# H split into a high and a low part as it leaves PSUM, stored as a pair and loaded straight into the operand ring; edges in 125 rows, loaded first; adjacency total on VectorE

## The chip, the core and the metric

The program runs on one core of a Trainium2 chip. The metric is the time of one execution in device microseconds (us). Three executions of the kernel before took 1498.07, 1499.3 and 1508.9 us; the median is 1499.3 us.

## The reference

A graph of 625 nodes with 1024 features goes through two layers; 20,625 edges (source, destination, one of 8 types) are given as three lists. What matters here is the first part, a relational graph convolution with a gate:

```python
x = x + L0_gnn(layernorm(x))        # this part
x = x + int8_ffn(layernorm(x))
x = x + gcn(layernorm(x))           # uses the sum of all adjacencies
x = x + mixture_of_experts(layernorm(x))

def L0_gnn(x):
    out = x @ root + bias
    for r in range(8):
        mask = (edge_type == r)
        sums = segment_sum(x[src] * mask, dst)
        cnt = segment_sum(mask, dst)
        out = out + (sums / max(cnt, 1)) @ weight[r]
    z = concat([out, x]) @ w_gate + b_gate
    return tanh(out) * z + x * (1 - z)
```

## The kernel before, in words

The mean over the edges and the product with a weight are exchanged. For each relation r, H_r = x @ weight[r] (625 x 1024) is computed first; then the adjacency of r (625 x 625, counts of edges) is multiplied by H_r, and each row is scaled by one over its count.

All f32 products run as products of numbers in the fp32r format. An operand is split in a high part (a copy to fp32r) and a low part (the rest); weights need three matmuls (high x high, low x high, high x low), the adjacency, whose numbers are small integers, needs two. The 625 nodes are 5 chunks of 125 rows, which stand on 125 partitions. Moving operands are tiles of 512 columns. A tile arrives by DMA in `stage` (two halves of up to four tiles, one DMA for each half, line 381), ScalarE copies its high part into `rh` (L330), VectorE subtracts and writes the low part into `rl` (L338). `rh` and `rl` are a ring of RT = 10 tiles: tile i may be written when tile i-10 has been used by TensorE.

**First stage, the units (L532 to L541).** Unit 0 is the root weight, units 1 to 8 the relations, unit 9 the gate's second half. A unit has two half-units (512 columns of the result each); a half-unit is 8 weight tiles x 5 chunks x 3 = 120 matmuls. Its five results stand in five of the eight PSUM banks. For units 1 to 8 ScalarE copies each to one of NHE = 6 slots `He` (L975), and its queue stores the slot in DRAM, `h_scratch` (L979). Unit 9 is added to a bias by VectorE (L1276), stored in `zx_scratch`, and read back later.

**Beside it: the edges.** The three edge lists are loaded by ScalarE's queue in pieces of 83, 78 and 1 rows (L939 to L941). Keys (destination, type, source as one number) are made from them, turned by TensorE, stored in DRAM, and read back in windows of 640 keys, each copied to 128 partitions (`KR`, L924). In each half-unit VectorE compares two windows (L1210, L1213), and GpSimd adds 165 columns of counts into `adj_scratch` in DRAM by indirect DMAs (L1759), in groups of five; a group waits for the one before it.

**Second stage, the spreads (L567 to L583).** For each relation and half, 5 tiles of H are loaded from `h_scratch` through `stage` (L381), split by ScalarE and VectorE, and multiplied with the adjacency, in 50 matmuls. The adjacency of a relation is loaded into `acb` (L396), copied by ScalarE into `Ar` (L934), and summed over sources by VectorE (L1289). GpSimd sums the eight adjacencies into `Atot` by eight DMAs that add (L1765). VectorE adds the scaled results to `U` (L1322). SP's queue issues all loads in program order.

After that come the gate (whose weights are loaded at the end of the second stage), the int8 layer, the second graph layer and the experts; the change doesn't touch them.

Of the kernel before, what the change touches and what calls it, by code (L numbers as in the profile page):

```python
# [17 lines left out]
P, C = 125, 5  # L18
# [5 lines left out]
KROWS = 83  # L24
EDGES0 = KROWS * 128
# [84 lines left out]
def gnn_ffn_kernel(nc, x, src, dst, typ, w_root, w_rel, w_gate, w_gnn, w_e1, w_e2, w_s1, w_s2, w_int8,  # L110
                   rbias, gbias, wscale, fbias, nbias, router, b1, b2, out):
    hd = nc.dram_tensor("h_scratch", (R, 2, P, C * 512), F32, kind="Internal").ap()
    zxd = nc.dram_tensor("zx_scratch", (2, P, C * 512), F32, kind="Internal").ap()
    xed = nc.dram_tensor("xe_scratch", (NSP, D), F32, kind="Internal").ap()
    eod = nc.dram_tensor("eo_scratch", (NS7 + 128, D), F32, kind="Internal").ap()
    keyd = nc.dram_tensor("key_scratch", (2 * KROWS, 128), F32, kind="Internal").ap()
# [5 lines left out]
    with ExitStack() as ctx:  # L122
# [19 lines left out]
        rh = sb("rh", [128, RT, 512], F32R)  # L142
        rl = sb("rl", [128, RT, 512], F32R)
# [40 lines left out]
        er = [sb(f"er{i}", [KROWS, 2, 128], I32, ph0) for i in range(3)]  # L184
        kr0 = sb("kr0", [KROWS, 2, 128], F32, ph0)
        kr1 = sb("kr1", [KROWS, 2, 128], F32, ph0)
        kc = sb("kc", [128, TILES], F32, ph0)
        KR = sb("KR", [128, 4, TG * 128], F32, ph0)
        EQ = sb("EQ", [128, TG, TG * 128], BF16, ph0)
        later = sb("later", [128, (2 * TG - 1) * 128], BF16, ph0)  # L190
        cnt = sb("cnt", [128, TILES], F32, ph0)
        kd1 = sb("kd1", [128, TILES], F32, ph0)
        idx = sb("idx", [128, TILES], I32, ph0)
        dum = sb("dum", [128, TG], F32, ph0)
        Z = sb("Z", [128, 1527], F32, ph0)
        sb("hole0", [128, 9875 + C * N - 5 * 256 - 4 * TILES - 4 * TG * 128 - TG * TG * 64 - (2 * TG - 1) * 64 - TG - 1527], F32, ph0)
        He = sb("He", [P, NHE, 512], F32, ph0)
# [71 lines left out]
        d_tot = count("adj_totalled", 16)  # L269
        d_zx, d_xl = count("zx_in", 16), count("x_again", 16)  # L270
# [8 lines left out]
        banks = Banks()  # L279

# [16 lines left out]
        for r in range(R):  # L297
            for hf in range(2):
                group(hd[r, hf][:, 0:1536], P, *[("h", r, hf, k) for k in range(3)])
                group(hd[r, hf][:, 1536:2560], P, *[("h", r, hf, k) for k in range(3, 5)])  # L300
# [23 lines left out]
        def high_parts(e, on, to, split):  # L324
            for i in range(split[0], min(to, len(tiles))):
                s, h, _ = places(i)
                on.wait_ge(*at("loaded", tiles[i][0]))
                if i >= RT:
                    on.wait_ge(*at("used", i - RT))
                e.copy(h, s).then_inc(*a_hi.up(("hi", i)))  # L330
            split[0] = max(split[0], min(to, len(tiles)))

        def low_parts(e, on, to, split, own):
            for i in range(split[0], min(to, len(tiles))):
                if (i in pool_lo) == (own is p_lo):
# [16 lines left out]
        sums = [slice(0, 4 * P), slice(4 * P, N)]  # L352
# [10 lines left out]
        h_last = [("h_out", unit, hf, c) for unit in (R - 1, R) for hf in range(2) for c in range(C)]  # L363
        h_out = [("h_out", R - 1, 1, c) for c in range(2, C)] + [("h_out", R, hf, c) for hf in range(2) for c in range(C)]


        def sync(e, on):
            def load(g):
# [7 lines left out]
                if name[0] == "h":  # L376
                    for c in range(C):
                        on.wait_ge(*at("h_out", name[1], name[2], c))
# [12 lines left out]
            def adjacency_in(r):  # L391
                on.wait_ge(*at("added", TILES - 1))
                on.wait_ge(*at("slot zero"))
                if r >= 2:
                    on.wait_ge(*at("adj", r - 2))
                e.dma_start(acr[r % 2], adjacency(r)).then_inc(*d_adj[r % 2].up(("acb", r)))  # L396

            for g in range(2, first("h", 0, 0, 0)):
# [4 lines left out]
            for r in range(R):  # L403
                for g in range(first("h", r, 0, 0), first("h", r, 0, 0) + 4):
                    if r == 0 and g == first("h", 0, 1, 0):
                        adjacency_in(0)
# [1553 lines left out]
```

## Time and profile before

| | |
|---|---|
| three executions | 1498.07, 1499.3, 1508.9 us |
| profiled execution: time / span | 1508.7 / 1506.9 us |
| TensorE matmul busy | 1147.6 us (76% of the span) |
| VectorE / ScalarE / GpSimd busy | 800.1 / 400.5 / 427.8 us |
| granted TensorE clock, mean | 0.885 |
| moved by DMA | 205.7 MB, 137 GB/s over the span |
| chain that ended last | TensorE 49%, DMA 23%, VectorE 14% |

The span is cut by eye into a start (to 99.7 us), the first stage (to about 634 us), the second stage (to about 1057 us) and the rest. "DMA share" is the mean busy share of the core's 16 DMA engines, so 0.31 is what five of sixteen give. A clock of 1.00 is 2.4 GHz, 0.50 is 1.2 GHz. In the chain of waits each line is a piece of the path that ended last: start, length, what it was.

### The profile page before, as it was taken

How to read it: one execution, taken by the hardware profiler on the slowest of the kernel's cores; microseconds unless marked ns; L12 is line 12 of the kernel's file. 1: busy time of each engine (PE TensorE's matmuls, PEld its weight loads, DVE VectorE, ACT ScalarE, POOL GpSimd, SP SyncE). 2: the span in 40 equal slices, each digit the busy share in tenths (PEclk: the TensorE clock that was granted, in tenths of full speed). 3: DMA queues.
4: the chain of work that ended last, by engine and by line, in shares of the span. 5: the costliest groups of instructions: out<-in, count | busy, mean ns of one | idle time of the engine just before them, and what ended most of it. 6: DMA issues, size and time to landing. Idle time of an engine off the chain costs nothing.

```text
span 1506.9 us, 13564 instructions
## 1 busy us (share of the span) xinstructions
PE 1147.6 (76%) x5123; PEld 903.3 (60%) x5123; DVE 800.1 (53%) x1226; ACT 400.5 (27%) x672; POOL 427.8 (28%) x294
## 2 busy tenths in 40 slices
PE   0489999999999999833612555667895999779893
PEld 0367777777777777622411444556664687658772
DVE  0579677678677651121302143444489646646545
ACT  0321322322322322100101022223254423315651
POOL 1226656656556551100000000000063500230023
PEclk9999999999999999967765877888897999979996
DMA  4764567765554554553443332223320110177846
GB/s 152 269 227 110 142 178 210 202 164 150 155 148 128 145 134 111 168 146 100 98 122 85 103 114 89 105 105 134 114 75 37 70 56 29 37 202 250 269 159 166
DMA packets 95586, 205.70 MB, mean 137 GB/s; under 512 B 43845, under 2 KB 44622, under 8 KB 87066
## 3 DMA queue, kind: packets, MB, share of 16 engines
q1 hardware_dynamic: 26796, 128.69, 25.0%
q0 software_dynamic: 51568, 41.88, 14.5%
q10 hardware_dynamic: 17150, 34.19, 6.4%
q8 instruction: 44, 0.72, 0.2%
q14 instruction: 28, 0.23, 0.1%
HBM read 148.66 MB, written 55.97 MB: 136 GB/s over the span
## 4 chain that ended last, share of the span: by engine, by line
PE 49%; DMA 23%; DVE 14%; SPq 3%; ACT 3%; ACTq 3%; issue 2%; POOL 2%; another core or an unknown queue 0%; POOLq 0%; DVEq 0%
PE ps L479 43%; DMA stage<-h_scratch 14%; SPq L381 3%; DMA stage<-in_w_e 3%; DVE rl L338 3%; ACTq L940 2%; DMA acb<-adj_scratch 2%; DVE U L1322 2%; DVE Sr L1289 2%; ACT Ar L934 1%; PE ps L740 1%; DVE st L1161 1%; PE ps L703 1%; DMA xe_scratch<-U,SI 1%; DMA G<-eo_scratch,SI 1%
## 5 line engine op out<-in xcount | busy, mean ns | idle before, releaser
L338 DVE TENSOR_TENSOR rl<-stage,rh 128x512 fp32r<-128x512 f32 (+1 forms) x330 | 220.9, 710 | 493.3 <-ACT rh L330 492.8
L330 ACT CAST rh<-stage 128x512 fp32r<-128x512 f32 (+1 forms) x344 | 203.9, 622 | 765.4 <-DMA stage<-h_scratch 336.9
L479 PE MATMUL ps<-rh,xTh 128*125 128x512 f32 x880 | 351.1, 399 | 11.3 <-DVE rl L338 8.7
L479 PE MATMUL ps<-rl,xTh 128*125 128x512 f32 x880 | 349.3, 397 | 0.0
L479 PE MATMUL ps<-rh,xTl 128*125 128x512 f32 x880 | 347.9, 395 | 0.0
L1759 POOL DMA_INDIRECT adj_scratch<-cnt,idx x165 | 277.7, 1683 | 233.8 <-DMA adj_scratch<-cnt,idx 87.0
L479 PE MATMUL ps<-rh,Ar 125*125 125x512 f32 x400 | 177.0, 442 | 40.1 <-DVE He L1276 28.7
L479 PEld LDWEIGHTS ps<-rh,xTh 128*125 128x125 f32 x880 | 164.5, 187 | 54.5 <-DVE rl L338 10.0
L479 PEld LDWEIGHTS ps<-rh,xTl 128*125 128x125 f32 x880 | 164.3, 187 | 42.5
L479 PEld LDWEIGHTS ps<-rl,xTh 128*125 128x125 f32 x880 | 164.3, 187 | 40.3
L479 PE MATMUL ps<-rl,Ar 125*125 125x512 f32 x400 | 172.6, 432 | 0.0
L554 PE MATMUL ps<-ones,Sr 125*125 125x2 f32 x40 | 9.1, 337 | 171.4 <-DVE Sr L1289 171.4
L1210 DVE SCALAR_TENSOR_TENSOR EQ<-KR,kc,later 128x640 bf16<-128x640 f32 x165 | 134.1, 878 | 0.0
L479 PEld LDWEIGHTS ps<-rh,Ar 125*125 125x125 f32 x400 | 84.7, 212 | 67.3 <-DVE He L1276 29.4
L1213 DVE TENSOR_REDUCE cnt<-EQ 128x5 f32<-128x3200 bf16 x33 | 115.1, 3487 | 1.1
L554 PEld LDWEIGHTS ps<-ones,Sr 125*125 125x125 f32 x40 | 8.6, 306 | 174.5 <-DVE Sr L1289 174.4
L1765 POOL DMA_DIRECT2D Atot<-adj_scratch x8 | 23.0, 2871 | 268.0 <-DMA Atot<-adj_scratch 203.1
L479 PEld LDWEIGHTS ps<-rl,Ar 125*125 125x125 f32 x400 | 84.0, 210 | 20.9 <-issue 0.3
L1778 POOL TENSOR_TENSOR ZX<-ZX,U 125x512 f32<-125x512 f32 x5 | 9.7, 1943 | 195.8 <-DVE U L1364 195.8
L975 ACT COPY He<-ps 125x512 f32<-125x512 f32 x80 | 46.9, 587 | 28.7 <-ACT He L975 13.6
L1322 DVE SCALAR_TENSOR_TENSOR U<-ps,rc,U 125x512 f32<-125x512 f32 x75 | 51.1, 744 | 5.1 <-PE ps L479 4.3
L338 POOL TENSOR_TENSOR rl<-stage,rh 128x512 fp32r<-128x512 f32 x14 | 17.5, 1273 | 85.7 <-ACT rh L330 85.7
(264 smaller groups left out, 1333.6 us busy)
## 6 DMA issues: line engine op xcount, KB each, us to landing
stage<-in_w_rel SPq DMA_DIRECT2D x32, 1024.0 KB
h_scratch<-He ACTq DMA_DIRECT2D x80, 250.0 KB
stage<-in_w_e SPq DMA_DIRECT2D x16, 1024.0 KB
adj_scratch<-Z POOLq DMA_DIRECT2D x16, 763.5 KB, 25.4
Atot<-adj_scratch POOLq DMA_DIRECT2D x8, 1525.9 KB, 40.3
acb<-adj_scratch SPq DMA_DIRECT2D x8, 1525.9 KB
stage<-h_scratch SPq DMA_DIRECT2D x16, 750.0 KB
KR<-key_scratch ACTq DMA_DIRECT2D x33, 320.0 KB
```

What stands on the lines that cost most here:

```text
L330: e.copy(h, s).then_inc(*a_hi.up(("hi", i)))
L338: e.tensor_tensor(l, s, h.bitcast(F32), ALU.subtract).then_inc(*own.up(("lo", i)))
L381: e.dma_start(stage[0:rows, g % 2, 0:n * 512], source).then_inc(*d_group[g % 2].up(("loaded", g)))
L479: ins = e.matmul(ps[0:P, b, :], a, m, start=first and n == 0, stop=last and n == len(parts) - 1)
L940: e.dma_start(er[i][0:78, 1, :], a[EDGES0:20608].rearrange("(p q) -> p q", q=128)).then_inc(*d_edge.up())
L975: e.copy(He[:, s % NHE, :], ps[0:P, banks.of["unit", unit, hf, c], :]).then_inc(*a_out.up(("he", unit, c, hf)))
L1210: e.scalar_tensor_tensor(out=EQ[:, j, :], in0=KR[:, g % 4, :], scalar=kc[:, t:t + 1], in1=later[:, j0:j0 + TG * 128], op0=ALU.is_equal, op ...
L1213: e.tensor_reduce(cnt[:, cols], EQ[:], AX, ALU.add).then_inc(*v_row.up(("cnt", g)))
L1289: e.tensor_tensor(Sr[:, r % 2, :], a[:, 0, :] if c == 1 else Sr[:, r % 2, :].bitcast(F32), a[:, c, :], ALU.add).then_inc(*v_row.up(("sourc ...
L1322: e.scalar_tensor_tensor(out=U[:, c, HALF[hf]], in0=ps[0:P, banks.of["spread", r, hf, c], :], scalar=rc[:, r, c:c + 1], in1=U[:, c, HALF[h ...
L1759: e.indirect_dma_start(accd, bass.IndirectOffsetOnAxis(ap=idx[:, n:n + 1], axis=0), cnt[:, n:n + 1], None, compute_op=ALU.add).then_inc(*d ...
L1765: e.dma_start(Atot[:], adjacency(r), accum_op=ALU.add if r else ALU.bypass).then_inc(*d_tot.up(("total", r)))
```

## The change

- H is split as it leaves PSUM: ScalarE copies the high part into slot `Hp[:, s, 0]`, VectorE subtracts it from the PSUM bank and writes the low part into `Hp[:, s, 1]`, and ScalarE's queue stores both, 4 KB in each of 125 rows, in `h_scratch`, which is twice as large. In ScalarE's program the five copies of a half-unit come first, then the five stores.
- The loads of H no longer pass `stage`: one DMA for each tile puts both parts into slot i % 10 of `ring` (`rh` and `rl` are its two halves), when tile i-10 has been used. ScalarE and VectorE do nothing for these tiles.
- Unit 9 is not stored in DRAM; VectorE leaves it in `He` or in `stage`, and ScalarE copies it to `ZX`. The gate's first weights are loaded in relations 3 and 4.
- The copy of adjacency 0 comes after all units in ScalarE's program, no longer ahead of the last half-unit.
- The edges are 125 rows of 165, the first three DMAs of SP's queue; x goes out in turns on SP's and ScalarE's queues. A window is 625 keys on 125 partitions.
- `Atot` is summed by VectorE from `acb` (seven additions of 125 x 3125); GpSimd's eight DMAs are gone. The load of adjacency r+1 goes out between the two halves of relation r.

```diff
-            for c in range(C):
+            for i, a in enumerate((src, dst, typ)):
+                e.dma_start(er[i][:], a.rearrange("(p t) -> p t", p=TK)).then_inc(*d_edge.up(("edges",)))
+            for c in (0, 2, 4):
                 e.dma_start(U[:, c, :], x_v[:, c, :]).then_inc(*d_x[c].up(("x", c)))
-                if c in (0, 1):
-                    load(c)
+                if c < 4:
+                    load(c // 2)
...
+            def h_in(r, hf):
+                for k in range(C):
+                    i = tile["h", r, hf, k]
+                    on.wait_ge(*at("h_out", r, hf, k))
+                    on.wait_ge(*at("used", i - RT))
+                    e.dma_start(ring[0:P, i % RT, :, :].bitcast(F32).rearrange("p a n -> p (a n)"), h_part(r, hf, k)).then_inc(*d_h[i % RT].up(("lo", i)))
...
+            h_in(0, 0)
+            adjacency_in(0)
+            adjacency_in(1)
+            h_in(0, 1)
+            for r in range(1, R):
+                h_in(r, 0)
+                if r + 1 < R:
+                    adjacency_in(r + 1)
+                h_in(r, 1)
...
-                    for c in range(C):
-                        if unit and unit <= R:
+                    if unit and unit <= R:
+                        for c in range(C):
                             on.wait_ge(*at("unit", unit, hf, c))
-                            if s >= NHE:
-                                on.wait_ge(*at("he slot", s - NHE))
-                            e.copy(He[:, s % NHE, :], ps[0:P, banks.of["unit", unit, hf, c], :]).then_inc(*a_out.up(("he", unit, c, hf)))
-                        if unit:
-                            to = (hd[unit - 1, hf] if unit <= R else zxd[hf]).rearrange("p (c n) -> p c n", c=C)
+                            if s + c >= NHE:
+                                on.wait_ge(*at("he slot", s + c - NHE))
+                            e.copy(Hp[:, (s + c) % NHE, 0, :], ps[0:P, banks.of["unit", unit, hf, c], :]).then_inc(*a_out.up(("he high", unit, c, hf)))
+                        for c in range(C):
                             on.wait_ge(*at("he", unit, c, hf))
-                            e.dma_start(to[:, c, :], He[:, s % NHE, :]).then_inc(*d_he[s % NHE].up(("he slot", s), ("h_out", unit - 1, hf, c)))
+                            e.dma_start(h_part(unit - 1, hf, c), Hp[:, s % NHE, :, :].bitcast(F32).rearrange("p a n -> p (a n)")).then_inc(
+                                *d_he[s % NHE].up(("he slot", s), ("h_out", unit - 1, hf, c)))
                             s += 1
...
+                        elif unit <= R:
+                            on.wait_ge(*at("he high", unit, c, hf))
+                            e.tensor_tensor(Hp[:, s % NHE, 1, :], ps[0:P, b, :], Hp[:, s % NHE, 0, :].bitcast(F32), ALU.subtract).then_inc(
+                                *v_out.up(("he", unit, c, hf)))
...
+            def add_total(r):
+                on.wait_ge(*at("acb", r - 1))
+                on.wait_ge(*at("acb", r))
+                if r > 1:
+                    on.wait_ge(*at("total", r - 1))
+                e.tensor_tensor(Atot[:].rearrange("p c i -> p (c i)"), acb[0][:] if r == 1 else Atot[:].rearrange("p c i -> p (c i)"), acb[r % 2][:],
+                                ALU.add).then_inc(*v_row.up(("total", r)))
...
-            for r in range(R):
-                on.wait_ge(*(at("total", r - 1) if r else at("added", TILES - 1)))
-                e.dma_start(Atot[:], adjacency(r), accum_op=ALU.add if r else ALU.bypass).then_inc(*d_tot.up(("total", r)))
```

ScalarE's queue at the end of a half-unit of the first stage, before (`He` are the slots, `h_scratch` is DRAM, `KR` the windows of keys, `rh` the ring's high parts):

```order
L975 COPY He<-ps 125x512 [waits h_out4,products_done]
L979 DMA h_scratch<-He 125x512 [waits act_evicted]
L975 COPY He<-ps 125x512 [waits h_out5,products_done]
L979 DMA h_scratch<-He 125x512 [waits act_evicted]
L975 COPY He<-ps 125x512 [waits h_out0,products_done]
L979 DMA h_scratch<-He 125x512 [waits act_evicted]
L975 COPY He<-ps 125x512 [waits h_out1,products_done]
L979 DMA h_scratch<-He 125x512 [waits act_evicted]
L975 COPY He<-ps 125x512 [waits h_out2,products_done]
L979 DMA h_scratch<-He 125x512 [waits act_evicted]
L330 CAST rh<-stage 128x512
L924 DMA KR<-key_scratch 128x640 [waits dve_done]
```

The same place now:

```order
L988 CAST Hp<-ps 125x512 [waits h_out4,products_done]
L988 CAST Hp<-ps 125x512 [waits h_out5,products_done]
L988 CAST Hp<-ps 125x512 [waits h_out0,products_done]
L988 CAST Hp<-ps 125x512 [waits h_out1,products_done]
L988 CAST Hp<-ps 125x512 [waits h_out2,products_done]
L991 DMA h_scratch<-Hp 125x1024 [waits dve_evicted] x5
L336 CAST ring<-stage 128x512
L935 DMA KR<-key_scratch 125x625 [waits dve_done]
```

The stores carry 1024 columns for 512, they wait for VectorE, and the load of the keys has 125 rows for 128.

SP's queue in the second stage, before (two halves of a relation and the adjacency of the one after next):

```order
L381 DMA stage<-h_scratch 125x1536 [waits h_out4,dve_low_parts,h_out5,act_high_parts,h_out0,h_out1,h_out2]
L381 DMA stage<-h_scratch 125x1024 [waits act_high_parts,dve_low_parts]
L381 DMA stage<-h_scratch 125x1536 [waits h_out3,dve_low_parts,h_out4,act_high_parts,h_out5,h_out0,h_out1]
L381 DMA stage<-h_scratch 125x1024 [waits act_high_parts,dve_low_parts]
L396 DMA acb<-adj_scratch 125x5x625 [waits act_done]
```

And now, one relation:

```order
L411 DMA ring<-h_scratch 125x1024 [waits products_done,h_out4]
L411 DMA ring<-h_scratch 125x1024 [waits products_done,h_out5]
L411 DMA ring<-h_scratch 125x1024 [waits products_done,h_out0]
L411 DMA ring<-h_scratch 125x1024 [waits products_done,h_out1]
L411 DMA ring<-h_scratch 125x1024 [waits products_done,h_out2]
L404 DMA acb<-adj_scratch 125x5x625 [waits dve_done,act_done]
L411 DMA ring<-h_scratch 125x1024 [waits products_done,h_out3]
L411 DMA ring<-h_scratch 125x1024 [waits products_done,h_out4]
```

The loads wait for TensorE (`products_done`) where they waited for the splitting engines, each tile has a DMA of its own, and a relation loads 10 x 125 x 1024 columns for 10 x 125 x 512.

## Rows read from the trace of the kernel before

**Rows 1.** The page, DMA issues: transfers, count, KB each, us to landing.

```profile
stage<-in_w_rel SPq DMA_DIRECT2D x32, 1024.0 KB
h_scratch<-He ACTq DMA_DIRECT2D x80, 250.0 KB
...
Atot<-adj_scratch POOLq DMA_DIRECT2D x8, 1525.9 KB, 40.3
acb<-adj_scratch SPq DMA_DIRECT2D x8, 1525.9 KB
stage<-h_scratch SPq DMA_DIRECT2D x16, 750.0 KB
KR<-key_scratch ACTq DMA_DIRECT2D x33, 320.0 KB
```

**Rows 2.** Windows: stretch, length, engines busy (instructions), clock, DMA share, GB/s.

```profile
12.00:36.00 24.00, 0.00 (x0) 0.00 (x0) 0.00 (x0) 0.00 (x0) 0.00 (x0) 1.00 0.32 129
52.00:58.00 6.00, 4.02 (x13) 3.06 (x12) 4.71 (x8) 3.22 (x6) 4.16 (x8) 1.00 1.03 373
99.70:627.00 527.30, 527.27 (x2261) 420.44 (x2262) 351.81 (x418) 136.11 (x225) 279.48 (x166) 1.00 0.56 154
408.00:463.40 55.40, 55.40 (x239) 44.17 (x239) 41.38 (x48) 15.78 (x26) 30.65 (x19) 1.00 0.53 144
584.00:604.00 20.00, 20.00 (x88) 15.97 (x87) 4.97 (x9) 3.56 (x6) 0.00 (x0) 1.00 0.32 130
634.00:1057.00 423.00, 210.17 (x791) 162.37 (x791) 130.57 (x212) 71.44 (x96) 20.11 (x11) 0.72 0.37 110
929.00:1046.00 117.00, 89.10 (x349) 70.78 (x349) 54.74 (x87) 29.60 (x39) 0.00 (x0) 0.83 0.29 109
```

**Rows 3.** Windows within a half-unit, while the stores of H are in flight.

```profile
444.00:446.00 2.00, 2.00 (x10) 1.61 (x9) 2.00 (x1) 0.07 (x1) 0.83 (x1) 1.00 0.33 127
```

**Rows 4.** Windows in the second stage, loads of adjacency and H.

```profile
974.00:978.00 4.00, 4.00 (x19) 3.20 (x18) 0.00 (x0) 0.11 (x1) 0.00 (x0) 1.00 0.32 129
...
982.00:986.00 4.00, 4.00 (x19) 3.15 (x19) 2.84 (x5) 0.00 (x0) 0.00 (x0) 1.00 0.32 126
```

**Rows 5.** Chain of waits, the start: start, length, what.

```profile
28.79 10.96 ACTq L940
39.78 5.43 DMA er<-in_typ
...
54.65 2.41 DVE rl L338 x4
```

**Rows 6.** Chain of waits, end of the second stage.

```profile
1040.22 10.67 DMA stage<-h_scratch
...
1053.27 4.28 PE ps L479 x10
...
1059.02 9.83 DMA stage<-in_w_gate
...
1071.02 1.90 PE ps L469 x8
...
1077.45 2.33 PE ps L479 x10
```

**Rows 7.** Single lines: duration ns min/median/max, first and last start.

```profile
L979 ACTq DMA_DIRECT2D h_scratch<-He x80: 256/277/4568, 155.1 to 578.2; - x80
L338 DVE TENSOR_TENSOR rl<-stage,rh x330: 677/685/1771, 54.6 to 1451.1; 128x512 fp32r<-128x512 f32 x125, 125x512 fp32r<-125x512 f32 x40
```

**Rows 8.** The page, costliest groups, an eviction on VectorE: busy, mean ns; idle before.

```profile
L1322 DVE SCALAR_TENSOR_TENSOR U<-ps,rc,U 125x512 f32<-125x512 f32 x75 | 51.1, 744 | 5.1 <-PE ps L479 4.3
```

**Rows 9.** The scatter-adds of GpSimd: the line, and its longest idle time.

```profile
L1759 POOL DMA_INDIRECT adj_scratch<-cnt,idx x165: 1541/1548/2188, 96.3 to 566.1; - x165
...
  DMA adj_scratch<-cnt,idx: 87.0, 20
```

More of the change, by code:

```diff
@@ L23 @@
 TG = 5
-KROWS = 83
-EDGES0 = KROWS * 128
+TK = E // TILES
 NG = TILES // TG
@@ L141, in gnn_ffn_kernel @@
         stage = sb("stage", [128, 2, SW], F32)
-        rh = sb("rh", [128, RT, 512], F32R)
-        rl = sb("rl", [128, RT, 512], F32R)
+        ring = sb("ring", [128, RT, 2, 512], F32R)
+        rh, rl = (ring[:, :, i, :] for i in range(2))
         EOs = sb("EOs", [HC, 3, D], F32, phx)
@@ L298, in gnn_ffn_kernel @@
             for hf in range(2):
-                group(hd[r, hf][:, 0:1536], P, *[("h", r, hf, k) for k in range(3)])
-                group(hd[r, hf][:, 1536:2560], P, *[("h", r, hf, k) for k in range(3, 5)])
+                for k in range(C):
+                    tile["h", r, hf, k] = len(tiles)
+                    tiles.append((None, 0, P))
         for hf in range(2):
@@ L334, in low_parts @@
             for i in range(split[0], min(to, len(tiles))):
-                if (i in pool_lo) == (own is p_lo):
+                if tiles[i][0] is not None and (i in pool_lo) == (own is p_lo):
                     s, h, l = places(i)
@@ L375, in load @@
                             on.wait_ge(*at("lo", i))
-                if name[0] == "h":
-                    for c in range(C):
-                        on.wait_ge(*at("h_out", name[1], name[2], c))
+                if name[0] == "gate" and g <= tiles[tile["gate", 0, 4]][0]:
+                    on.wait_ge(*at("zx copied", 1))
                 if g in (tiles[tile["e1", 2, 0]][0], tiles[tile["e2", 0, 0, 0]][0]):
@@ L519, in tensor @@
             nothing = lambda c: None
[L522 to L528 removed]
+            b, freed = banks.take(("keys",), ("key rows",))
+            on.wait_ge(*at("key columns"))
+            on.wait_ge(*at("ident"))
+            for ev in freed:
+                on.wait_ge(*at(*ev))
+            e.transpose(ps[:, b, 0:TK], kc[:, 0:128], ident[0:TK, 0:TK]).then_inc(*product.up())
+            e.transpose(ps[0:TILES - 128, b, TK:2 * TK], kc[:, 128:TILES], ident[0:TK, 0:TK]).then_inc(*product.up(("keys turned",)))
             banks.drop(("keys",))
@@ L960, in scalar @@
                 for hf in range(2):
-                    if unit == R + 1 and hf == 1:
-                        adjacency_copy(0)
                     if unit or hf:
@@ L993, in scalar @@
+            for hf in range(2):
+                for c in range(C):
+                    on.wait_ge(*at("he", R + 1, c, hf))
+                    on.wait_ge(*at("unit", R + 1, 1, C - 1))
+                    e.copy(ZX[:, c, HALF[hf]], zx_place(c, hf)).then_inc(*a_row.up(("zx copied", hf)))
+            for r in range(R):
+                if r + 1 < R:
+                    adjacency_copy(r + 1)
+                if 3 <= r <= 7:
+                    c = r - 3
                     on.wait_ge(*at("x again"))
@@ L1345, in vector @@
                 many_vector(e, Waiter(e))
-            lows(tile["h", R - 1, 1, 0] + RT)
+            lows(tile["gate", 0, 5])
             for c in range(C):
```

189 lines of the change are left out of this document (80 added, 109 removed).

## The prediction

> **What bounds the kernel now.** I read the windows first, then the sizes of the transfers, then the chain of waits, and the single lines last.
>
> In the first stage TensorE is busy without a gap: 2261 matmuls in 527.3 us, 0.233 us each, so 27.7 to 28 us for a half-unit's 120 [rows 2]. In the second it is busy 210 of 423 us, at a mean clock of 0.72, while the DMA share is 0.37 at 110 GB/s [rows 2]. That looks like idle DMA engines. It isn't. The reader should put three windows side by side: 12 to 36 us, where only x and the two biases (125 rows each) are on their way, runs at a share of 0.32 and 129 GB/s; 584 to 604, loads and stores of H together, 0.32 and 130 GB/s; 52 to 58, with 128-row transfers, 1.03 and 373 GB/s [rows 2]. In the middle of the first stage, stores of H: 0.33, 127 [rows 3]. In the second, adjacency and H: 0.32 to 0.33 at 126 to 129 [rows 4]. So everything with 125 rows goes through five of the sixteen engines, at about 130 GB/s together whichever queue it comes from, and mixing loads and stores or queues adds nothing. The account to keep is that of these five.
>
> In the steady first stage the mean engine works 0.53 x 27.7 = 14.7 us of a half-unit [rows 2]. H's store is 5 x 250 KB = 1.28 MB [rows 1], 9.85 us on five engines, 3.1 as a mean of sixteen. The rest, 11.6 us, lies on all (weights, windows of keys, scatter-adds). The five have 9.85 + 11.6 = 21.5 us of work in 27.7. In the last three relations of the second stage, 117 us [rows 2], a relation takes 39 us and holds 2.56 + 1.56 MB [rows 1], 31.7 us at 130 GB/s: 81% busy.
>
> **The start.** The keys wait for the edges until 45.2 us, through the slow issue of the pieces on ScalarE's queue [rows 5]; the fourth low part ends at 57. Now the edges are first, 0.25 MB, and should be there by 8 us. Then x and weights bound the start: ahead of the second weight group the five engines carry the edges, x chunks 0 and 2, and 1 and 3 from the other queue, 2.3 MB or 18 us, and two weight groups, 2.1 MB at 373 GB/s or 6 us; it lands at about 27 us, and was used at about 60. I take 30 us saved; the ends are 0 (ScalarE caught in the issue of its two loads) and 37 (x chunk 0 alone decides).
>
> **The first stage.** H's store doubles: 2.56 MB, 19.7 us on the five. The windows of keys had 128 rows, 0.66 MB at 373 GB/s, 1.8 us of every engine; now they have 125, 0.62 MB at 130, 4.8 us of the five. New load of the five in a half-unit: 19.7 + 11.6 - 1.8 + 4.8 = 34.3 us, where TensorE wants 27.7. Six slots of H hold a little over one half-unit, so the excess soon reaches the PSUM banks. VectorE isn't the bound: it is busy 41.4 in two half-units, 20.7 in one [rows 2], and gets 5 subtractions more, at the price of an eviction, 0.744 us [rows 8], 3.7 us: 24.4 of 27.7. ScalarE waits for them before it stores, but has a whole half-unit of tiles split ahead.
>
> The first store was issued at 155.1 [rows 7], now at 125. Fifteen intervals of 34.3 us and a last batch of 19.7 us give 659 us for the last store. TensorE alone would have issued that batch at 125 + 15 x 27.7 = 540.
>
> **The second stage.** What the five still have to move then: H, 2 x 20.5 = 41 MB at 130 GB/s, 315 us; eight adjacencies, 12.5 MB, 98 us; x again, 2.56 MB, 20 us; two groups of gate weights, 6 us. Sum 439 us. The first loads of H may go out while TensorE is in its last half-unit, and the ring has room for ten tiles, so I let the five run through: the last tile of H lands at 659 + 439 = 1098. At full clock TensorE needs 800 x 0.233 = 186 us there and at half clock (ten in 4.28 against 2.33 us [rows 6]) 342; neither bounds. VectorE loses 80 low parts of 0.685 us [rows 7] and gets seven additions, which I bound from five lines of the eviction's kind, 5 x 0.744 = 3.7 us, 26 us in all, under cover of the loads. GpSimd's eight adding DMAs, 40.3 us each [rows 1], go. Relations with them beside took (929 - 634) / 5 = 59 us, those without 39 [rows 2], so this removal is worth up to 100 us; H's doubling takes it back: a relation is now 5.12 + 1.56 MB, 51.4 us at 130 GB/s.
>
> **The end.** The last load of H landed at 1050.9; two chunks of matmuls later, and after 13.5 us for gate weights, the first turn came at 1071.0 [rows 6]. Now these weights are there: last landing, 4.3 + 3.7 us of matmuls, turn. The rest, 1506.9 - 1071.0 = 436 us, is unchanged. Span = 1098 + 8 + 436 = 1542, with 1.8 us around it 1544, against the profiled execution's 1508.7: +35. Against the median of 1499.3 that is 1535.
>
> **A rule of the skill against the rows.** The Trainium skill, "DMA: Bandwidth & Descriptors", section "Issuing engines are not separate DMA queues", says that DMAs of all queues run on the same 16 engines, and its section "Measured (HBM→SBUF, 128 partitions, SWDGE, issued from GpSimd)" has 341 GB/s for 1 MB. Taken alone these would hide H's doubling. The same page, section "Why a DMA increments its semaphore by 16 and not by 1", says that the number of engines is the largest up to 16 that divides the outer dimensions on both sides; for 125 that is 5. By that rule the trace agrees: 0.32 of 16 is five [rows 2].
>
> **Rivals.**
> - *All sixteen carry the new transfers* (the first rule above). Units end at 634 - 30 = 604, the second stage is TensorE's 186 us: 604 + 186 + 8 + 436, 1226 on the median's scale. Against it stand all windows of rows 2 to 4. Chance 0.02.
> - *Faster: the first stage stays TensorE's.* The five would have to do 34.3 us of work in 27.7, say because rows of 4 KB move faster than those of 2 KB. Units end at 604, loads of H start 35 us earlier: last landing 569 + 439 = 1008, span 1452, on the median's scale 1445. It decides at a load of 27.7 us, 160 GB/s on five engines; x has rows of 4 KB and ran at 129 [rows 2]. Chance 0.12.
> - *Slower still: the scatter-adds are late.* A group is 5 x (1.548 + 0.3) = 9.3 us of issue and a wait, 87 us over 20 waits before [rows 9]; first to last start, 470 us for 33 groups, 14.2 us each. A half-unit of 34.3 us allows 17.1. If the waits grow in engines that are never free, to 20 us a group, they end at about 70 + 660 = 730, and the adjacency, on which SP's queue stands with H behind it, was due at 665: +65, 1600. Chance 0.12.
> - *The start saves nothing:* the first store stays at 155, +30, 1565. Chance 0.10.
> - *The clock:* in gaps it falls, and 120 matmuls at half clock need 51 us, above 34.3. If it stayed there, +16 x 17. A busy TensorE got it back within a few us before. Chance 0.03.
>
> **The numbers.** My forecast has 0.61, and its own range is 1500 to 1575: 3% on a rate of 130 GB/s is 25 us, and gaps in the five's work can only add. This measurement tells about 1% from no change. Faster by over 1% (under 1484): 0.02 + 0.12 and a tail of 0.01, 0.15. Within 1% (up to 1514): the forecast's lower end, 0.15. Slower: 0.70. The range of 8 in 10 leaves out the fast rivals and the far end of the slow ones: 1475 to 1600.
>
> **What would show it.** In the changed kernel's profile: the first matmul at 20 to 27 us for 55; the first store of H near 125; in the first stage a DMA share of at least 0.5 that never falls under 0.31, gaps in TensorE where it had none, 34 us for a half-unit, and ScalarE waiting for the slots or standing in its issue of stores; the last store near 660; in the second stage a share of 0.31 to 0.33 at 130 GB/s throughout, 51 us for a relation, TensorE waiting for `ring`; the gate with no wait for weights. Wrong it would be if the share in the first stage fell to 0.31 between stores and TensorE stayed without gaps, or if H's rows moved at another rate than 130 GB/s.

## The result, and the profile after

The changed kernel takes 1732.9 us (median of 4 runs, 1725.7 to 1742.2), the kernel before, run beside it, 1504.1: a ratio of 1.152, 95% interval 1.142 to 1.162. Forecast were 1535 us, and a range of 1475 to 1600. The sign was right, the size was not: 198 us are missing.

Its profiled execution has a span of 1724.3 us. The page, its 40 slices and its queues (packets, MB, share of sixteen engines' span):

```profile
PE   2899888789889899000055535465549789897994
...
POOL 2054224232422426776600000000003540131004
PEclk8999999889999999555578967888879889997996
DMA  6845556554554553111133333333330211037846
GB/s 199 342 119 155 174 177 189 183 177 157 172 168 150 164 170 84 1 1 1 1 127 129 130 130 141 130 141 130 130 129 26 97 51 59 26 105 224 272 169 177
...
q0 software_dynamic: 81312, 29.65, 9.5%
q10 hardware_dynamic: 15132, 52.38, 7.9%
```

Look at slices 17 to 20, counted from 1. TensorE is at 0, nothing moves (1 GB/s), yet the DMA engines show a share of a tenth, and GpSimd is at its busiest, 6 and 7. Something small is late. The windows, in the columns of [rows 2]:

```profile
75.70:688.00 612.30, 554.40 (x2280) 437.52 (x2280) 396.99 (x505) 123.83 (x224) 216.90 (x104) 0.95 0.52 162
400.00:500.00 100.00, 92.41 (x385) 72.80 (x384) 72.35 (x92) 21.82 (x40) 37.05 (x18) 0.97 0.54 168
696.00:856.00 160.00, 0.00 (x0) 0.00 (x0) 0.00 (x0) 0.00 (x0) 114.51 (x59) 0.50 0.15 1
900.00:950.00 50.00, 27.27 (x102) 19.67 (x103) 13.69 (x17) 2.80 (x1) 0.00 (x0) 0.86 0.32 130
```

The first stage runs from 75.7 to 688 and its 2280 matmuls fill 91% of it. Then comes a hole of 160 us, in which only GpSimd works, on 59 instructions. The second stage is as forecast: 0.32 at 130 GB/s. What GpSimd does in the hole is the scatter-adds, line L1773, which answers to [rows 9]; beside it the casts that fill H's slots:

```profile
L1773 POOL DMA_INDIRECT adj_scratch<-cnt,idx x165: 1977/1986/2695, 94.3 to 857.3; - x165
its engine sat idle before it (us, times) until:
  DMA adj_scratch<-cnt,idx: 219.8, 21
  issue: 120.0, 138
```
```profile
L988 ACT CAST Hp<-ps x80: 577/597/624, 131.6 to 630.8; 125x512 fp32r<-125x512 f32 x80
```

Both begin as early as before, or earlier (94.3 for 96.3 us). But the last scatter-add is issued at 857.3 us, where it was 566.1 [rows 9]; one takes 1986 ns to issue for 1548, and the waits for the adding DMAs are 219.8 us for 87.0. TensorE's and ScalarE's first stage was over some 170 us earlier. The chain of waits through the hole (start, length, what) repeats one pattern, the issues of a group, 0.3 us apart, and then a wait of 3.6 us:

```profile
746.19 3.63 DMA adj_scratch<-cnt,idx
...
750.67 1.99 POOL adj_scratch L1773
752.65 0.30 issue
752.96 1.98 POOL adj_scratch L1773
...
759.82 3.55 DMA adj_scratch<-cnt,idx
```

A group of five takes 759.82 - 746.19 = 13.6 us there, with nothing else running. While H is being stored it costs more than twice that. GpSimd in order of time (start, length, what, idle before it and its releaser):

```profile
408.60 1.98 POOL L1773 DMA_INDIRECT adj_scratch<-cnt,idx  x1 [0.30 <-issue]
429.42 1.99 POOL L1773 DMA_INDIRECT adj_scratch<-cnt,idx  x1 [18.83 <-DMA adj_scratch<-cnt,idx]
...
439.68 1.99 POOL L1773 DMA_INDIRECT adj_scratch<-cnt,idx  x1 [0.30 <-issue]
462.39 1.98 POOL L1773 DMA_INDIRECT adj_scratch<-cnt,idx  x1 [20.72 <-issue]
```

From 429.42 to 462.39 is one group: 33 us. The releaser of the second wait is given as "issue", but it lies at the same place of the loop, before the first scatter-add of a group, where the program waits for the group before. From the first store of H to the last the mean of 14 groups is 32.9 us; over the whole run it is (857.3 - 94.3) / 32.8 = 23.3 us, for 14.3 before (32 whole groups and the four issues of the last make 32.8).

Did VectorE deliver the counts too late? A group needs its indices, which VectorE writes. Their lines, before and after (first and last start):

```profile
L1219 DVE TENSOR_TENSOR idx<-kd,dum x33: 164/166/168, 95.9 to 543.3; 128x5 int32<-128x5 f32 x33
```
```profile
L1233 DVE TENSOR_TENSOR idx<-kd,dum x33: 164/165/196, 71.8 to 601.4; 125x5 int32<-125x5 f32 x33
```

Now the last indices are written at 601.4 us and the last scatter-add goes out 256 us later, so VectorE isn't the cause. Before, the first twenty groups each started within some 3 us of their indices, which came every (543.3 - 95.9) / 32 = 14.0 us. The 14.3 us of before are for the most part VectorE's pace, not the price of a group.

Who waits for the last scatter-add is SyncE. The first adjacency is issued at 860.9, and all but five of H's loads stand behind it (the queue of SyncE: start, time until the last of the row is issued, what, how many):

```profile
655.26 14.26 SPq L411 DMA_DIRECT2D ring<-h_scratch  x5
```
```profile
860.89 5.10 SPq L404 DMA_DIRECT2D acb<-adj_scratch  x2
910.33 3.50 SPq L404 DMA_DIRECT2D acb<-adj_scratch  x1
913.92 47.66 SPq L411 DMA_DIRECT2D ring<-h_scratch  x10
961.63 3.54 SPq L404 DMA_DIRECT2D acb<-adj_scratch  x1
```

From one adjacency to the next it is 961.63 - 910.33 = 51.3 us: a relation's price in the forecast was 51.4. (The next one, which also loads x, takes 71.3, the two with gate weights 55.7 and 57.0, the last 51.4.) The end of that stage in the chain of waits, which answers to [rows 6]:

```profile
1263.74 26.34 DMA ring<-h_scratch
1290.12 4.47 PE ps L488 x12
1294.59 0.85 PE ps L478 x8
1295.44 2.32 PE ps L488 x10
```

No wait for gate weights is left, as forecast.

### The profile page after: what moved, and what is told of

Same layout as the page of the kernel before. It is cut to its first block, busy times and chain, and to the rows that moved or that the text cites. A ratio compares the mean times of both kernels' runs of the same rounds, so it can differ in the third digit from the quotient of the medians.

```text
span 1724.3 us, 13452 instructions
## 1 busy us (share of the span) xinstructions
PE 1174.0 (68%) x5123; PEld 907.3 (53%) x5123; DVE 812.9 (47%) x1229; ACT 350.0 (20%) x604; POOL 465.6 (27%) x285
## 3 DMA queue, kind: packets, MB, share of 16 engines
q0 software_dynamic: 81312, 29.65, 9.5%
q10 hardware_dynamic: 15132, 52.38, 7.9%
## 4 chain that ended last, share of the span: by engine, by line
SPq 23%; DMA 21%; DVE 17%; PE 14%; POOL 12%; ACTq 5%; issue 5%; ACT 2%; POOLq 0%; DVEq 0%
SPq L411 21%; DMA adj_scratch<-cnt,idx 12%; POOL adj_scratch L1773 11%; PE ps L488 9%; ACTq L991 5%; DVE EQ L1224 3%; DVE ring L344 3%; DVE cnt L1227 3%; DMA stage<-in_w_e 2%; SPq L404 2%; DMA ring<-h_scratch 2%; DVE Hp L1284 1%; PE ps L751 1%; PE ps L714 1%; DMA G<-eo_scratch,SI 1%
## 5 line engine op out<-in xcount | busy, mean ns | idle before, releaser
L488 PE MATMUL ps<-ring,xTh 128*125 128x512 f32 x1760 | 573.6, 408 | 71.0 <-DVE Hp L1284 56.5
L488 PE MATMUL ps<-ring,Ar 125*125 125x512 f32 x800 | 229.1, 439 | 383.1 <-issue 192.4
L1773 POOL DMA_INDIRECT adj_scratch<-cnt,idx x165 | 339.7, 2059 | 475.1 <-DMA adj_scratch<-cnt,idx 219.8
L488 PEld LDWEIGHTS ps<-ring,xTh 128*125 128x125 f32 x1760 | 336.7, 193 | 161.6 <-DVE Hp L1284 62.0
L488 PEld LDWEIGHTS ps<-ring,Ar 125*125 125x125 f32 x800 | 159.3, 207 | 448.8 <-DMA ring<-h_scratch 219.7
L488 PE MATMUL ps<-ring,xTl 128*125 128x512 f32 x880 | 354.5, 403 | 0.0
L344 DVE TENSOR_TENSOR ring<-stage,ring 128x512 fp32r<-128x512 f32 x250 | 167.3, 717 | 238.8 <-ACT ring L336 233.4
L336 ACT CAST ring<-stage 128x512 fp32r<-128x512 f32 x264 | 153.4, 624 | 554.7 <-issue 183.7
L488 PEld LDWEIGHTS ps<-ring,xTl 128*125 128x125 f32 x880 | 169.0, 192 | 44.1
L1224 DVE SCALAR_TENSOR_TENSOR EQ<-KR,kc,later 125x625 bf16<-125x625 f32 x165 | 131.6, 867 | 0.0
L1227 DVE TENSOR_REDUCE cnt<-EQ 125x5 f32<-125x3125 bf16 x33 | 112.5, 3408 | 1.1
```

Of the source, the lines that this page charges most:

```text
L344: e.tensor_tensor(l, s, h.bitcast(F32), ALU.subtract).then_inc(*own.up(("lo", i)))
L488: ins = e.matmul(ps[0:P, b, :], a, m, start=first and n == 0, stop=last and n == len(parts) - 1)
L1224: e.scalar_tensor_tensor(out=EQ[:, j, :], in0=KR[:, g % 4, :], scalar=kc[:, t:t + 1], in1=later[:, j0:j0 + TG * TK], op0=ALU.is_equal, op1 ...
L1227: e.tensor_reduce(cnt[:, cols], EQ[:], AX, ALU.add).then_inc(*v_row.up(("cnt", g)))
L1773: e.indirect_dma_start(accd, bass.IndirectOffsetOnAxis(ap=idx[:, n:n + 1], axis=0), cnt[:, n:n + 1], None, compute_op=ALU.add).then_inc(*d ...
```

## The experiments

Four kernels form a square: the rows of the scatter-adds (125 or 128) by the rows in which H is stored and loaded (125 or 128). Rows added to reach 128 hold zeros, and the scatter-adds' extra rows add zero to dummy places. The edits are the same throughout.

**Scatter-adds in 128 rows.** The changed kernel, with three more rows for the scatter-adds alone:

```diff
-        cnt = sb("cnt", [TK, TILES], F32, ph0)
+        cnt = sb("cnt", [128, TILES], F32, ph0)
...
-        idx = sb("idx", [TK, TILES], I32, ph0)
+        idx = sb("idx", [128, TILES], I32, ph0)
...
+            e.memset(cnt[:], 0.0).then_inc(*p_row.up())
+            e.tensor_copy(idx[:].rearrange("p (g t) -> p g t", t=TG), dum[:].unsqueeze(1).broadcast_to([128, NG, TG])).then_inc(*p_row.up(("pad rows",)))
```

> The changed kernel, with the scatter-adds in 128 rows again (three rows add 0 to places of their own); H still moves in 125 rows. Theory A (the five engines are so full of H's stores that each group of scatter-adds waits about 20 us for its last landing): a group still has parts on the five full engines, so groups stay near 30 us while H is stored, the last scatter-add starts later than 750 us, and the time stays over 1640 us. Theory B (a scatter-add in 125 rows is slow by itself, since it runs on five engines and takes 2.06 us to issue instead of 1.68): groups return to about 14 us, the last scatter-add starts before 600 us, and the time falls by about 190 us to 1540.

Measured: 1540.0 us, ratio to the kernel before 1.021 (1.016 to 1.026). Three rows more in 165 small DMAs give back 193 us. The line of the scatter-adds:

```profile
L1777 POOL DMA_INDIRECT adj_scratch<-cnt,idx x165: 1532/1542/2179, 94.5 to 658.6; - x165
its engine sat idle before it (us, times) until:
  DMA adj_scratch<-cnt,idx: 183.8, 25
```

The last one goes out 198.7 us earlier, and the issue is back at 1542 ns. The adjacency is asked for at 666.4 (forecast 665), when SyncE has issued the first five loads of H. H's last landing is at 1075.6 + 25.7 = 1101.4 (forecast 1098), the span is 1536.3 (forecast 1542). This is the kernel that my sum described. Of the two theories B had the time, and neither had the scatter-adds: the last one starts at 658.6, where A said later than 750 and B before 600.

**H in 128 rows.** The changed kernel, its scatter-adds left at 125 rows, H's tiles and its place in memory with 128 rows:

```diff
-    hd = nc.dram_tensor("h_scratch", (R, 2, P, C * 1024), F32, kind="Internal").ap()
+    hd = nc.dram_tensor("h_scratch", (R, 2, 128, C * 1024), F32, kind="Internal").ap()
...
-        Hp = sb("Hp", [P, NHE, 2, 512], F32R, ph0)
+        Hp = sb("Hp", [128, NHE, 2, 512], F32R, ph0)
```

> The changed kernel, with H stored and loaded in 128 rows (three of zeros), so that it should use all sixteen engines; scatter-adds still in 125 rows. Theory A: the five engines are free, the waits of the groups shrink to a few us, the last scatter-add starts before 640 us; the units take 28 us for a half-unit and end near 610; the second stage is bound by TensorE or by the adjacency on five engines, 190 to 230 us; time 1250 to 1330 us. Theory B: groups stay at 25 to 30 us, the last scatter-add starts after 800 us, and the second stage begins only there: time about 1500 us.

Measured: two runs, 29 us apart, 1359 and 1388 us, so no ratio is given; the trace is of the longer one. The last scatter-add is at 656.5 us, with an issue of still 1987 ns. Theory A had forecast it before 640 and the time at 1250 to 1330, theory B after 800 and about 1500: neither fits, A is the nearer. So the lateness has two causes.

**Both.**

> Both edits: H and the scatter-adds in 128 rows. Both theories: the scatter-adds are done before the units end (about 610 us), the second stage takes 190 to 230 us, and the time is 1240 to 1320 us. Theory A expects no more than 15 us between this and H in 128 rows alone; theory B expects some 200 us.

Measured: 1317.7 us, ratio 0.873 (0.870 to 0.877), last scatter-add at 554.1. The change that was 15% slower has become one that is 13% faster, with the same arithmetic. Against this kernel either cause alone makes the last scatter-add 102 to 105 us later, and both together 303, about 100 more than the sum of the two: each makes the other worse. Between this kernel and the one before it theory A expected no more than 15 us and B some 200; measured are 41 and 70.

**The kernel before, scatter-adds in 125 rows.** It leaves out the edges in the last three rows:

```diff
-                e.indirect_dma_start(accd, bass.IndirectOffsetOnAxis(ap=idx[:, n:n + 1], axis=0), cnt[:, n:n + 1], None,
+                e.indirect_dma_start(accd, bass.IndirectOffsetOnAxis(ap=idx[0:P, n:n + 1], axis=0), cnt[0:P, n:n + 1], None,
```

> The kernel before, with its scatter-adds in 125 rows instead of 128; the edges of the last three rows of each column are left out of the adjacency, nothing else differs. The price of the rows by themselves, with H's stores on the five engines at half of the changed kernel's size. Theory A: issue grows from 1.68 to 2.06 us, waits by a few us; a group takes 14 to 17 us instead of 14.2, and the time moves by less than 40 us. Theory B: a group takes 25 us or more, the last scatter-add starts after 800 us, and the time rises by over 150 us.

Measured: 1614.8 us, ratio 1.070 (1.066 to 1.075), last scatter-add at 710.9. That is 106 us more, where theory A had less than 40 and theory B over 150. The 125 rows do harm without anything else of the change, beside stores of H of half the size. The square, with the kernel before and this one below it:

```
rows of scatter / of H      last scatter-add   mean group   time
125 / 125 (the change)      857.3 us           23.3 us      1733 us
128 / 125                   658.6              17.2         1540
125 / 128                   656.5              17.1         1359 and 1388
128 / 128                   554.1              14.0         1318
before, 128 / 125, H once   566.1              14.3         1504 to 1512
before, 125 / 125, H once   710.9              18.7         1615
```

**The total alone.** The kernel before, with the seven additions on VectorE and without GpSimd's eight adding DMAs:

```diff
-            for r in range(R):
-                on.wait_ge(*(at("total", r - 1) if r else at("added", TILES - 1)))
-                e.dma_start(Atot[:], adjacency(r), accum_op=ALU.add if r else ALU.bypass).then_inc(*d_tot.up(("total", r)))
...
+                e.tensor_tensor(Atot[:].rearrange("p c i -> p (c i)"), acb[0][:] if r == 1 else Atot[:].rearrange("p c i -> p (c i)"), acb[r % 2][:],
+                                ALU.add).then_inc(*v_row.up(("total", r)))
```

> The kernel before, with the total of the adjacencies summed by VectorE and without GpSimd's eight adding DMAs: one part of the change alone. If these DMAs are what made the first five relations take 59 us instead of 39, the gain is near 100 us: 1400 to 1430. If the relations are slow there for another reason (stores of unit 9, H and adjacency on five engines), the gain is under 50 us: over 1455.

Measured: 1427.7 us, ratio 0.944 (0.941 to 0.948), 84 us less than the 1511.7 beside it. That is the part of the change worth having; the forecast gave it "up to 100". Against it the 128 / 125 kernel, which has all of the change but the 125 rows of the scatter-adds, stands at 1.021: the ratios differ by 0.077, or 116 us. So the rest of the change took back at least that, and what the start saves (24 us) on top. The rest is H's doubling and also the windows of keys in 125 rows, which in the forecast's account add 4.8 - 1.8 = 3.0 us to the five engines' half-unit, where the doubling adds 9.85. No run parts the two.

**H in 128 rows in the kernel before,** once alone and once with the total on VectorE:

```diff
-    hd = nc.dram_tensor("h_scratch", (R, 2, P, C * 512), F32, kind="Internal").ap()
+    hd = nc.dram_tensor("h_scratch", (R, 2, 128, C * 512), F32, kind="Internal").ap()
...
-        He = sb("He", [P, NHE, 512], F32, ph0)
+        He = sb("He", [128, NHE, 512], F32, ph0)
```

> The kernel before, with H stored and loaded in 128 rows, one f32 number for each element as before. The five engines' account says that 20.5 MB each way leave them: a relation without GpSimd's DMAs beside it falls from 39 to 28 to 32 us, the others from 59 to 45 to 50, the time to 1390 to 1440. If the time is not a matter of five engines, it stays within 20 us of 1504.

> The kernel before with both: H in 128 rows and the total on VectorE. It has neither H's doubling nor the early edges. If doubling H pays for itself by taking the split off ScalarE and VectorE, this is over 1385; if it doesn't, this is at 1318 + 24 (start) + 13 (gate weights), 1355 or below.

Measured: 1414.1 us (0.935, 0.932 to 0.939) and 1366.0 (0.903, 0.900 to 0.907). The first is inside its forecast of 1390 to 1440. Together the two edits save 146 us and not 98 + 84 = 182: what they relieve overlaps. It isn't the five engines alone: while GpSimd's adding DMAs of 125 rows were on their way, the share in the kernel before rose above what five of sixteen can give:

```profile
640.00:660.00 20.00, 0.00 (x0) 0.00 (x0) 1.87 (x3) 1.66 (x3) 0.00 (x0) 0.50 0.69 161
```

The second kernel lies between the two theories' numbers and decides for neither. With the earlier start (24 us) and without the wait for gate weights (13.5 us in the prediction) it would be at about 1328, an estimate; the 128 / 128 kernel, which stores and loads twice the bytes of H, has 1318. So with H in 128 rows its doubling costs nothing that shows.

**Everything on sixteen engines.** The 128 / 128 kernel, with the windows of keys in 128 rows too, and adjacency, x and biases each as a DMA of 112 rows and one of 13:

```diff
...
-                e.dma_start(acr[r % 2], adjacency(r)).then_inc(*d_adj[r % 2].up(("acb", r)))
+                for a, b in ((0, 112), (112, P)):
+                    e.dma_start(acr[r % 2][a:b], adjacency(r)[a:b]).then_inc(*d_adj[r % 2].up(("acb", r)))
...
```

> The changed kernel with every large transfer made to use all sixteen engines: H, scatter-adds and windows of keys in 128 rows, adjacency, x and the first two biases in two DMAs of 112 and 13 rows. If the second stage is bound by bytes on the five engines (adjacency), a relation falls from 32 us to TensorE's 24 and the time to 1240 to 1265. If it is bound by waits (the landing of a tile, the clock after a gap), it stays near 30 us for a relation and the time at 1295 to 1315.

Measured: 1231.2 us, ratio 0.815 (0.812 to 0.818), the best of all, and 9 us under the lower end of its forecast: the second stage was bound by bytes. Its windows over the first stage and in the second:

```profile
69.80:602.00 532.20, 532.17 (x2280) 424.33 (x2281) 402.94 (x501) 138.74 (x225) 273.08 (x164) 1.00 0.66 192
...
600.00:780.00 180.00, 177.68 (x784) 141.78 (x783) 102.15 (x135) 33.41 (x26) 2.02 (x5) 1.00 0.98 299
```

No gap in the first stage, and a second stage in which TensorE is busy 177.7 of 180 us while the DMA share is 0.98 at 299 GB/s. Both resources are full; what is left to gain there is little.

**The edges late again,** in that kernel: the three loads behind x and the biases.

```diff
-            for i, a in enumerate((src, dst, typ)):
-                e.dma_start(er[i][:], a.rearrange("(p t) -> p t", p=TK)).then_inc(*d_edge.up(("edges",)))
             for c in (0, 2, 4):
...
+            for i, a in enumerate((src, dst, typ)):
+                e.dma_start(er[i][:], a.rearrange("(p t) -> p t", p=TK)).then_inc(*d_edge.up(("edges",)))
```

> The version with everything on sixteen engines (1231 us), but the edges loaded after x and the biases instead of before them. If the early load of the edges is what brings the start forward there: the keys and with them the last scatter-add come 15 to 25 us later; the time 1245 to 1260, if the scatter-adds' end sets when the second stage can begin. Rival: with sixteen engines x and the weights are no longer ahead of the edges for long, and the first matmul hangs on them anyway: under 8 us of difference, 1225 to 1239.

Measured: 1247.6 us, 16.4 us more, as forecast. The interval of the ratio, 0.812 to 0.836, is wide and reaches the other kernel's; it is the traces that carry the reading. The edges land at 27.0 us and not at 10.2 (the chains' first rows, of the one with early edges and of this one), the first store of H goes out at 147.7 and not at 127.6, and the last scatter-add is issued 20 us later:

```profile
1.57 8.61 DMA er<-in_typ
```
```profile
9.00 18.01 DMA er<-in_typ
```

**Stores with smaller packets.** Why does a wait for scatter-adds last 20 us beside H's stores, when it lasts 3.6 without them? The changed kernel, each store as two DMAs with rows of 2 KB:

```diff
-                            e.dma_start(h_part(unit - 1, hf, c), Hp[:, s % NHE, :, :].bitcast(F32).rearrange("p a n -> p (a n)")).then_inc(
-                                *d_he[s % NHE].up(("he slot", s), ("h_out", unit - 1, hf, c)))
+                            for a in range(2):
+                                e.dma_start(h_part(unit - 1, hf, c)[:, a * 512:(a + 1) * 512], Hp[:, s % NHE, a, :].bitcast(F32)).then_inc(
+                                    *d_he[s % NHE].up(("he slot", s), ("h_out", unit - 1, hf, c)))
```

> The changed kernel, each store of H (125 rows of 4 KB) issued as two DMAs of 125 rows of 2 KB, high parts and low parts; the same bytes on the same five engines. Theory T (turns): on an engine the scatter's small packets take turns with the store's packets, so a wait costs one store packet for each of its descriptors. The mean wait before a group was about 20 us with packets of 4 KB; with packets of 2 KB it falls to about 11, a group to about 15 to 20 us, the last scatter-add starts at 650 to 750 us instead of 857, and the time is 1540 to 1640. Rival F (fullness): the scatter waits because the five engines have too many bytes to move, whatever their packets; the bytes are the same, so groups stay at 23 us, the last scatter-add at about 857, the time 1715 to 1750.

Measured: 1642.3 us, ratio 1.084 (1.068 to 1.100): 90 us less than the change, with the same bytes on the same engines. The bytes alone don't set the wait. GpSimd, in the same stretch as above:

```profile
405.73 1.99 POOL L1774 DMA_INDIRECT adj_scratch<-cnt,idx  x1 [6.34 <-DMA adj_scratch<-cnt,idx]
...
422.50 1.99 POOL L1774 DMA_INDIRECT adj_scratch<-cnt,idx  x1 [10.19 <-issue]
...
436.03 2.11 POOL L1774 DMA_INDIRECT adj_scratch<-cnt,idx  x1 [8.82 <-DVE EQ L1225]
...
456.97 1.99 POOL L1774 DMA_INDIRECT adj_scratch<-cnt,idx  x1 [9.33 <-DMA adj_scratch<-cnt,idx]
```

The 10.19 us lie inside a group, after its third scatter-add, and what ends them isn't named; such a pause comes four times in every kernel with scatter-adds of 125 rows. The waits before a group are 6 to 9 us here, where they were 19 and 21. For 100 to 600 us, the waits of GpSimd that the profile puts down to the group before (total, times, longest), in the change, with 2 KB, and in the kernel before with scatter-adds of 125 rows:

```profile
POOL adj_scratch L1773 <- DMA adj_scratch<-cnt,idx: 158.5, 9, 25.2
```
```profile
POOL adj_scratch L1774 <- DMA adj_scratch<-cnt,idx: 105.3, 12, 14.9
```
```profile
POOL adj_scratch L1759 <- DMA adj_scratch<-cnt,idx: 74.4, 10, 12.3
```

A mean wait is 17.6, 8.8 and 7.4 us. The third kernel stores half the bytes of the second, in rows of 2 KB as well, and waits nearly as long: the length of the rows moves the wait far more than the bytes do. The theory of turns had about 11. Two of its numbers were missed by little: the last scatter-add is at 772.3 us (650 to 750 expected), the time 2 us outside. My sum for it was wrong, since five issues of 2.29 us and a wait of 10 make 21 us for a group, not 15 to 20; measured, 20.7. And there is a cost that I had left out. ScalarE now issues twice as many stores, and stands longer in it (before the change's row, after this kernel's):

```profile
411.24 10.08 ACTq L991 DMA_DIRECT2D h_scratch<-Hp  x5
```
```profile
406.16 16.25 ACTq L992 DMA_DIRECT2D h_scratch<-Hp  x10
```

Its last store is at 710.6 us for 634.5. What the theory says of the mechanism goes as follows. The packets of ScalarE's queue take a mean 0.079 x 16 x 1724.3 / 15132 = 0.144 us in the change, and 0.088 x 16 x 1635.9 / 25532 = 0.090 with 2 KB:

```profile
q10 hardware_dynamic: 25532, 52.38, 8.8%
```

(These means also count the windows of keys, whose packets are the same in both.) If a group of 5 x 25 rows on an engine lets one such packet pass at each row, it waits 125 x 0.144 = 18.0 us, and 11.3 with 2 KB; in 128 rows, 5 x 8 on an engine, 5.8. Measured: 17.6, 8.8, and 183.8 / 25 = 7.4 in the 128 / 125 kernel. That is an estimate that fits in size, not a proof: that a scatter-add of 125 rows puts 25 on each of five engines is an assumption. The Trainium skill, "DMA: Bandwidth & Descriptors", section "Queues, rings and completion order", says that an engine serves its queues in turn, and changes between them only at the end of a packet. The trace agrees as far as it goes: with packets of half the bytes the wait is half as long. How many turns a row takes isn't seen. A scatter-add of 125 rows leaves (81312 - 36432) / 165 = 272 packets more than one of 128, whose queue has (29.65 - 29.29) MB less, so 8 bytes for each of them; the 128 / 125 kernel's queue:

```profile
q0 software_dynamic: 36432, 29.29, 9.9%
```

## Why the prediction was wrong, point by point

**The failed step: the load of the scatter-adds,** in the part on what bounds the kernel and again in "The first stage". I wrote that everything with 125 rows goes through five engines, and then put the scatter-adds, which the change brings from 128 rows to 125, among the work that "lies on all", at their old price. The diff shows their new shape in `cnt` and `idx`. The rival "the scatter-adds are late" was the right mechanism: waits that grow in engines that are never free, SyncE standing in front of the adjacency with H behind it. It had a chance of 0.12 and was priced at 20 us a group and +65, because I took the issue at its old 9.3 us and let the waits alone grow. Measured are 23.3 us a group and 860.9 - 665 = +196 us at the first adjacency. Of the 291 us by which the last scatter-add moved, 339.7 - 277.7 = 62 are issue (GpSimd's busy time in all 165, by the two pages), and the rest, 229, waits. Undoing the 125 rows of the scatter-adds alone moves the time from 1733 to 1540: the miss of 198 us, nearly whole.

A rule of the skill that I used for H covers this as well, and I didn't carry it over. The Trainium skill's "DMA: Bandwidth & Descriptors", section "Why a DMA increments its semaphore by 16 and not by 1", gives its rule for the number of engines for DMAs of GpSimd too, with exceptions. No row here shows which engines a scatter-add used; the runs show that its price depends on 125 or 128. Nor do all DMAs of 125 rows keep to five engines, as the prediction had it: the share of 0.69 beside GpSimd's adding DMAs speaks against it.

**The sum, term by term,** in the profiled executions:

```
                                        forecast    measured
first matmul                            20 to 27    27.2 us
continuous TensorE, saved               30          99.7 - 75.7 = 24.0
half-unit of the first stage            34.3        (630.8 - 131.6 - 2.0) / 15 = 33.1
last packet of H's stores               659         655.8
first adjacency                         665         860.9
one relation of the second stage        51.4        51.3
last landing of H                       1098        1290.1
from there to the first turn            8           4.5
rest                                    436         1724.3 - 1294.6 = 429.7
span                                    1542        1724.3
```

(In the half-unit, 2.0 us are the other four casts of the last batch. The 659 is nearly right by errors that cancel: the first store came 9 us later than forecast and the last batch took 4 to 5 longer, fifteen half-units took 17 less. The eight adjacencies in the sum are 12.5 MB, 96 us at 130 GB/s and not 98.) The span is off by 182 us: 192 at the last landing, less 3.5 and 6.3. The other 16 of the 198 lie between profiled executions and medians.

**The account of five engines held** for what SyncE and ScalarE move. The half-unit was 3% too long in the forecast, the relation exact, the share and rate in the second stage 0.32 and 130 GB/s as read from [rows 2], VectorE and TensorE bounded nothing. TensorE waits for `Hp` (56.5 us in all) and ScalarE stands in the issue of its stores, as forecast. That the windows of keys went to five engines as well is inside the 33.1. With the scatter-adds at their old price the sum gives 1535, and the run that gives them back their 128 rows has 1540.

**The start** was forecast well in its size and not in its way. The edges land at 15.6 us, not 8: on SyncE's queue they are first, but x chunks go out beside them on ScalarE's. That these share their engines is likely, not shown; where x and the other large transfers use all sixteen, the edges land at 10.2. The first store goes out at 134.4 for 125, the first cast at 131.6. That the early edges matter at all is shown in the last pair: 16.4 us.

**The other rivals.** "All sixteen carry the new transfers" gave 1226 us. It was no description of this kernel, but of the one in which the large transfers do go by sixteen, all but 13 rows of some: 1231. The clock fell to 0.50 in the hole, when TensorE had nothing to do, and was back at a mean of 0.86 in the window from 900 us on; it caused none of it, with TensorE busy 27.3 of 50 us in that window. "The start saves nothing" was refuted by the 24 us.

**The profile could have told it:** [rows 9] had the scatter-adds' issue and waits, and from its last start, 566.1, to my 665 there were 99 us of slack, 3 us a group. I compared 14.2 us a group with the 17.1 that a half-unit allows and stopped there, without asking what the new rows do to the 14.2, nor whether it was a price at all: it was in the main the pace at which VectorE delivered.

## What to carry to other kernels

When a change alters the number of rows of a tile, list every DMA that reads or writes it, the small ones too, and price each anew: here 165 scatter-adds of half a kilobyte cost 193 us because they had 125 rows, more than the doubling of H (41 MB) and the keys in 125 rows together (116, or 140 with the start). Where five of sixteen engines carry the load, try padding to 128 rows, or a split into 112 and 13: the ratio of 1.15 became 0.87 with the first and 0.81 with both. A time between two starts is a price only where nothing else sets the pace: look at what the engine waited for. And how long a small DMA waits beside a large stream depended here on the length of the stream's packets, not on its bytes alone.

## What the runs showed of the hardware

- A scatter-add of 125 rows takes GpSimd 1986 ns to issue, one of 128 rows 1542, and the one of 125 leaves 272 more packets, of 8 bytes; a group of five of 125 rows takes 13.6 us with nothing beside it.
- The mean wait of a group of scatter-adds beside H's stores fell from 17.6 us to 8.8 when the stores' rows went from 4 KB to 2 KB at equal bytes, and was 7.4 with rows of 2 KB and half the bytes.
- Issuing stores is not free: 5 stores of 500 KB held ScalarE for 10.1 us, 10 of 250 KB for 16.3, and SyncE needed 47.66 / 10 = 4.8 us for each load of H while five engines were behind.
- With H, keys and scatter-adds in 128 rows and the rest split into 112 and 13, transfers ran at 299 GB/s for 180 us beside a TensorE busy 99% of the time at full clock.
